# A mixture-of-experts pipeline on one core: halves joined plane by plane, swish read from PSUM, hid turned one step behind its product, and a counter for each product

## The reference

```python
    x = x + 0.5 * _L0_ffn_ref(_layernorm(x), ...)
    x = x + _L0_attn_ref(_layernorm(x), ...)
    x = x + 0.5 * _L0_ffn_ref(_layernorm(x), ...)

def _swiglu(h):
    glu = jnp.minimum(h[..., ::2], LIMIT)          # LIMIT = 7.0
    lin = jnp.clip(h[..., 1::2], -LIMIT, LIMIT)
    return glu * jax.nn.sigmoid(ALPHA * glu) * (lin + 1.0)

# expert block: 32 experts, 4 chosen for each token
        t = _rmsnorm(x, norm_scale)
        g = t @ gate_w.T + gate_b
        vals, idx = jax.lax.top_k(gf, K)
        w = jax.nn.softmax(vals, axis=-1)
        combine = jnp.zeros((T, E)).at[jnp.arange(T)[:, None], idx].add(w)
        h1 = jnp.einsum('th,efh->tef', tf, w1) + b1
        h = _swiglu(h1)
        hw = h * combine[:, :, None]
        out = jnp.einsum('tef,ehf->th', hw, w2) + combine @ b2
        return x + out
```

## Time and profile before

| | us |
|---|---|
| median of 3 runs | 711.7 (710.67 to 713.89) |
| time of the profiled execution | 712.26 |
| its span, first to last instruction | 710.5 |
| POOL busy | 507.7 (71%) |
| PE busy | 504.9 (71%) |
| ACT busy | 455.6 (64%) |
| DVE busy | 436.0 (61%) |

### The profile page before, as it was taken

The page is one execution under the profiler, slowest core; times in us unless marked ns, Lnnn a source line. Parts: engine busy times, 40 slices in busy tenths (PEclk is TensorE's granted clock), DMA queues, the critical chain, the costliest instruction groups (busy, mean ns, idle before and its releaser), DMA issues. The chain is left out here.

```text
span 710.5 us, 11944 instructions
## 1 busy us (share of the span) xinstructions
PE 504.9 (71%) x2868; PEld 408.8 (58%) x2869; DVE 436.0 (61%) x1243; ACT 455.6 (64%) x784; POOL 507.7 (71%) x551
## 2 busy tenths in 40 slices
PE   6258977999979997595507864699997999935000
PEld 3144364889868886264404552388896988834000
DVE  6889232665548778388983877155663787845122
ACT  4848425999879897595807747399986999711000
POOL 3677777777557776777677777777763777777765
PEclk9556999999999999697558955899999999957555
DMA  7998115787569995122121111578766999624222
GB/s 268 394 368 319 52 53 126 194 218 212 183 160 192 223 220 177 45 54 56 45 55 52 53 53 52 112 172 220 206 197 158 206 211 221 178 75 126 66 63 59
DMA packets 144043, 108.25 MB, mean 152 GB/s; under 512 B 112416, under 2 KB 119808, under 8 KB 143872
## 3 DMA queue, kind: packets, MB, share of 16 engines
q1 hardware_dynamic: 127616, 74.14, 39.2%
q0 software_dynamic: 16384, 33.59, 16.4%
HBM read 25.84 MB, written 56.62 MB: 116 GB/s over the span
## 5 line engine op out<-in xcount | busy, mean ns | idle before, releaser
L570 POOL DMA_INDIRECT YG<-ys,row x256 | 247.3, 966 | 104.1 <-issue 98.0
L545 POOL DMA_INDIRECT xs<-planes,row x256 | 249.9, 976 | 81.4 <-issue 71.3
L1321 PE MATMUL PS<-W,xT 128*128 x768 | 192.2, 395 | 17.8 <-ACT xT L659 16.4
L1321 PEld LDWEIGHTS PS<-W,xT 128*128 128x128 f32 x768 | 141.8, 194 | 46.5 <-issue 28.5
L659 ACT ACTIVATE xT<-xP 128x1024 uint16<-128x1024 uint16 x96 | 144.8, 1512 | 36.3 <-DMA xP<-xs 36.2
L1019 DVE TENSOR_SCALAR glulin<-PS 128x512 f32<-128x512 f32 x96 | 66.3, 691 | 124.2 <-PE PS L1330 70.6
L1330 PEld LDWEIGHTS PS<-W,hidT 128*128 128x128 f32 x768 | 99.9, 191 | 6.1 <-issue 1.6
L1330 PE MATMUL PS<-W,hidT 128*128 x768 | 101.7, 276 | 0.5 <-issue 0.5
L650 ACT ACTIVATE swish<-glulin 128x512 f32<-128x512 f32 x96 | 60.4, 629 | 23.1 <-DVE glulin L1019 17.9
L1032 DVE SCALAR_TENSOR_TENSOR hid<-glulin,swish 128x512 f32<-128x512 f32 x96 | 66.4, 692 | 11.9 <-ACT swish L650 5.6
L1024 DVE TENSOR_SCALAR glulin<-PS 128x512 f32<-128x512 f32 x96 | 65.3, 681 | 0.0
(11 more groups left out here) (178 smaller groups left out, 690.1 us busy)
## 6 DMA issues: line engine op xcount, KB each, us to landing
ys<-yrow SPq DMA_DIRECT2D x96, 256.0 KB
xs<-YG SPq DMA_DIRECT2D x6, 2048.0 KB, 14.0
W<-in_w12T SPq DMA_DIRECT2D x1, 6144.0 KB, 34.4
xs<-planes,row POOLq DMA_INDIRECT x256
YG<-ys,row POOLq DMA_INDIRECT x256, 2.5
out<-X SPq DMA_DIRECT2D x7, 256.0 KB, 2.5
xP<-xs SPq DMA_TRANSPOSE x96
X<-in_x SPq DMA_DIRECT2D x4, 256.0 KB, 3.3
```

The source lines that it names most:

```text
L545: pool.indirect_dma_start(out=xs[c].bitcast(U16), out_offset=bass.IndirectOffsetOnAxis(ap=row[:, i:i + 1], axis=0), in_=planes[:, (c * CT ...
L570: pool.indirect_dma_start(out=YG[:, t * TOPK + k, :], out_offset=None, in_=ys[c], in_offset=bass.IndirectOffsetOnAxis(ap=row[:, i:i + 1], ...
L1321: last = te.matmul(h1, xT[:, r, q * P:(q + 1) * P], W[:, bass.ds(es[q], 2 * H)], start=True, stop=True)
```

## The change

- **Join.** The copy that puts the halves together walks through all low halves of the 512 numbers and then through all high halves. Before, it took the low and the high half of each number in turn.
- **Swish.** ACT reads the first product in PSUM itself and computes the swish of the unbounded number. The bound is put on the result: DVE takes the smaller of swish and `cap`, which holds the swish of 7, in the instruction that makes `hid`. So `glu` is gone, DVE does two instructions for a group in place of three. `lin` waits until the swish has read, and `hid` waits for `lin`. The 1 that is added to `lin` is folded into the bias b1 once at the start, and the bounds are -6 and 8.
- **Order.** PE does in step k: first product of k-1, turn of k-2, second product of k-3. ACT does: y copy of k-4, join of k, swish of k-1, copy to `hidT` of k-2. SP's order, `STORE_LAG` and the waits of its loads and stores stay as they are.
- **Counts.** `h1_ready` counts first products and `y_ready` second products, in place of `multiplied` and `seam_multiplied`. ACT and DVE can read the first product before the second product of the same step is done.
- At the start of the first block ACT computes `cap`, and the load of its table goes with it. The loops of DVE are cut in another way, with the same work in each step.

The core of the diff:

```diff
@@ scalar, experts @@
                 def copy_y(n, r, m):
+                    act.wait_ge(y_ready, n + (g0 + 1))
                     wait_count(act, yrow_stored[r], (m + (g0 // 2)) * 16)
                     a.activation(yrow[:, r, :], YP[r], ACT.Copy).then_inc(yrow_ready, 1)
 
                 def swish_of(n, r):
-                    act.wait_ge(glu_ready, n + (g0 + 1))
+                    act.wait_ge(h1_ready, n + (g0 + 1))
                     wait_count(act, hid_ready, n + (g0 - 1))
-                    a.activation(swish[:, r, :], glu[:, r, :], ACT.Gelu_apprx_sigmoid).then_inc(swish_ready, 1)
+                    a.activation(swish[:, r, :].rearrange("p (q f) -> p q f", q=GT),
+                                 H1[r].rearrange("p (q g f) -> p g q f", q=GT, g=2)[:, 0],
+                                 ACT.Gelu_apprx_sigmoid).then_inc(swish_ready, 1)
 
                 def copy_hid(n, r):
                     act.wait_ge(turned, n + (g0 + 1))
+                    wait_count(act, y_ready, n + (g0 - 1))
                     a.activation(hidT[:, r, :], HT[r], ACT.Copy).then_inc(hidT_ready, 1)
...
-                    wait_count(act, multiplied, n + (m0 - 1))
-                    a.activation(xT[:, r, :].bitcast(U16).rearrange("p (q n w) -> p q n w", q=GT, w=2),
-                                 xP[:, r, :].rearrange("p (w n q) -> p q n w", q=GT, w=2), ACT.Copy).then_inc(xT_ready, 1)
+                    wait_count(act, h1_ready, n + (g0 - 1))
+                    a.activation(xT[:, r, :].bitcast(U16).rearrange("p (q n w) -> p w q n", q=GT, w=2),
+                                 xP[:, r, :].rearrange("p (w n q) -> p w q n", q=GT, w=2), ACT.Copy).then_inc(xT_ready, 1)
...
-                    if live(k, 5, NGF) and not (isinstance(k, int) and NG + 3 <= k <= NG + 4):
-                        act.wait_ge(multiplied, k + (m0 - 1))
-                        copy_y(k - 5, s, m - (3 if r == 0 else 2))
-                    if live(k, 2, NGF):
-                        swish_of(k - 2, r)
-                    if live(k, 3, NGF):
-                        wait_count(act, multiplied, k + (m0 - 1))
-                        copy_hid(k - 3, s)
-                    join_rows(k, r, m)
+                    behind_seam = isinstance(k, int) and k > NG
+                    if live(k, 4, NGF) and not (behind_seam and k - 4 < NG):
+                        copy_y(k - 4, r, m - 2)
+                    if live(k, 0, NGF) and not (isinstance(k, int) and k == NG + 1):
+                        join(k, r, m)
+                    if live(k, 1, NGF):
+                        swish_of(k - 1, s)
+                    if live(k, 2, NGF) and not (behind_seam and k - 2 < NG):
+                        copy_hid(k - 2, r)
@@ vector, experts @@
-                        dve.wait_ge(multiplied, k + m0)
-                        wait_count(dve, swish_ready, k + (g0 - 2))
-                        v.tensor_scalar(glu[:, s, :].rearrange("p (q f) -> p q f", q=GT), h1[:, 0],
-                                        LIMIT, None, ALU.min).then_inc(glu_ready, 1)
+                        dve.wait_ge(swish_ready, k + g0)
+                        wait_count(dve, hid_ready, k + (g0 - 2))
+                        v.tensor_scalar(lin[:, s, :].rearrange("p (q f) -> p q f", q=GT), h1[:, 1],
+                                        1 - LIMIT, 1 + LIMIT, ALU.max, ALU.min).then_inc(lin_ready, 1)
                     add(1)
                     if live(k, 1, NGF):
-                        wait_count(dve, hid_ready, k + (g0 - 2))
-                        v.tensor_scalar(lin[:, s, :].rearrange("p (q f) -> p q f", q=GT), h1[:, 1],
-                                        -LIMIT, LIMIT, ALU.max, ALU.min).then_inc(lin_ready, 1)
+                        dve.wait_ge(lin_ready, k + g0)
+                        wait_count(dve, turned, k + (g0 - 2))
+                        v.scalar_tensor_tensor(hid[:, s, :], swish[:, s, :], cap[:, 0:1], lin[:, s, :], ALU.min, ALU.mult)\
+                            .then_inc(hid_ready, 1)
@@ tensor, experts @@
                 def step(k, r):
-                    if live(k, 3, NGF):
-                        turn_hid(k - 3, 1 - r)
+                    s = 1 - r
+                    behind_seam = isinstance(k, int) and k > NG
                     if live(k, 1, NGF):
-                        last = first_product(k - 1, 1 - r)
-                        if live(k, 4, NGF) and not (isinstance(k, int) and k == NG + 3):
-                            last = second_product(k - 4, r)
-                        last.then_inc(multiplied, 1)
+                        first_product(k - 1, s)
+                    if live(k, 2, NGF) and not (behind_seam and k - 2 < NG):
+                        turn_hid(k - 2, r)
+                    if live(k, 3, NGF) and not (behind_seam and k - 3 < NG):
+                        second_product(k - 3, s)
```

More of the change, by code:

```diff
@@ L719, in experts @@
                         step(i * 4 + (8 + j), j % 2, i * 2 + (8 + j) // 2)
[L720 to L721 removed]
+                drain(NG)
+                join(NG, 0, NG // 2)
+                join(NG + 1, 1, NG // 2)
+                for k in range(NG + 1, NG + 8):
                     step(k, k % 2, k // 2)
```

114 lines of the change are left out of this document (35 added, 79 removed).

## The result

The changed kernel takes 718.07 us (median of 6 runs, 717.61 to 721.3), the kernel before 711.85 (710.53 to 713.89). The ratio is 1.0086, with a 95% interval of 1.0068 to 1.0104: slower by 6.2 us. The prediction was 712.0 with a range from 707.4 to 717.0; the measured time lies above it. What happened is in the main what its second rival described, the store as the new wait, with a part of the third, a join that gets less short than taken. The profiled execution took 717.92 us, with a span of 716.2.

A forecast was written before the change was run, and what follows sets the result against it. POOL's indirect DMAs were taken as the bound, so only its waits, 4.1 us, could be had. Block 1 0.1 us earlier and block 2 0.2 later made +0.1: 711.8, given as 712.0 us, range 707.4 to 717.0.

The forecast's parts named there:

- second rival: Y copy's store becomes the new wait: at 3.4 us a step, 5.1 us more, 716.8 us; chance 0.21.
- third rival: Join on ACT doesn't get shorter, its 16-bit output being stepped: 3.4 to 3.5 us a step, 717 to 720 us; chance 0.07.
- limit of 4.1 us from the four gaps: POOL's waits before gathers 0 to 3: most that faster experts can bring, 2.66 + 0.86 + 0.59 = 4.1 us.
- an earlier end of the experts changes nothing there: First block's seam, before gather 0: stores land behind loads that wait for scatter 1, so no gain there.
- limit of 0.86 us: Second block's seam, before gather 2: a wait of 10.33 us against 9.47, so at most 0.86 us can be had.
- gap before gather 0: POOL's wait at the first seam: unchanged at 9.5 us; a move of over 1 us would make the whole reading wrong.
- the sum: Second half-stages: 1.5 us gained minus 21 times the step's growth; with the second seam's 0.86, +0.1 us together.
- first rival: Stores land in time, steps of 3.15 us or less, gathers 1 and 3 without a gap: 4.1 us less, 707.6; chance 0.22.
- `yrow` ring: Two-step loop of join, load, store issue, landing and y copy: 6.6 us, 3.28 a step in the second half-stages.
- In the first half-stages 3.1 to 3.2: Pace of the experts' steps in each block's first half-stage, claimed at 3.1 to 3.2 us a step.
- fill and drain: Start and end of a half-stage: 0.5 us less at the start and 1.0 us less at the end.
- The path from a first product to `hid` stays as long: Swish part: swish, lin, hid in place of glu, swish, hid, claimed equally long, and begun earlier by the second product.

The follow-up runs named there:

- a_lag5: The changed kernel with STORE_LAG 5 in place of 6, each store issued one group earlier: 710.81 us, ratio 0.9948 to the kernel before.
- a_storefirst_4: The changed kernel with SP issuing the store of k-6 ahead of the load of k, fourth try: 710.36 us, ratio 0.9966 to the kernel before.
- a_best_3: The changed kernel with four yrow buffers, STORE_LAG 5 and POOL's wait for xT_ready one group back, third try: 709.99 us, ratio 0.9966 to the kernel before.
- j_steps: The changed kernel with 21 more copies on ACT before its first step, in seven access patterns: plain 1.051 us, the new join's 1.343, the old join's 1.504.
- a_y4: The changed kernel with four yrow buffers in place of two, order and STORE_LAG 6 kept: 711.25 us, ratio 0.9952 to the kernel before.

## Why the prediction was wrong

**What bounds the kernel.** Right in the main thing: no version gained more than 4.3 us by its ratio (3.4 by its median), near the limit of 4.1 us from the four gaps, and a_lag5 closed the gaps before gathers 1 and 3 to 0.30. One-sided at the seams: "an earlier end of the experts changes nothing there" holds, but a later one costs its whole length beyond the 0.6 us that the experts had to spare. For the second seam the limit of 0.86 us was too tight: the gap before gather 2 fell from 10.33 to 8.8 in a_storefirst_4 and to 8.4 in a_best_3. The prediction named a change of over 1 us in the gap before gather 0 as a sign that the reading is wrong as a whole. The gap grew by 1.94. What was wrong is this one half of it: the sum has no term for late experts in the first half-stages. It also has small slips that don't change the outcome: a landing of 3.3 us makes a step of 3.32 and not 3.29, the first rival is 707.6 in one place and 707.4 in another, and 3.5 a step in the third rival makes 721 and not 720.

**The join, the first step that failed.** I took 1.06 us, bounds 1.06 and 1.51, and said that the two-element run is what differs. It took 1.355: the row L624 has a stepped input and a contiguous output, the new join a stepped output, and that costs 0.29 us by j_steps. The two-element run alone, with input steps of 2 bytes, costs only 0.12. So the reason of the third rival ("its 16-bit output is now stepped", 0.07) was right, and its size was not: the join got shorter by 0.16 of the 0.45 us. By the prediction's own sum of the `yrow` ring, 0.29 more over two steps is 0.15 a step; 42 steps of the second half-stages make 6.2 us, and 712.0 would have been 718.2. That this meets the measured total is half chance: the steps in question grew by less, and the rest came from where the sum had nothing, as the next points show. The rule of the Trainium skill (SBUF — State Buffer, Door 1) of two hits in each 16-byte line nearly held for the input: 8-byte steps, two 16-bit numbers in a line, cost 0.06 us. For the output it doesn't give the price: 4-byte steps have four in a line and cost 0.29.

**The ring of `yrow`.** Its mechanism was right: the number of buffers, the lag of the store, SP's order and the join were each changed, and each moved the time in the direction that the ring says. It was the second rival, with 0.21. The second half-stages got 3.34 and 3.35 where I had 3.28, less than the 3.43 that the dearer join would give in that sum. The landing wasn't too long: where the y copy waited for its store, it took 3.4 us in the mean, from the start of the store's issue (2.4 to 5.3). But the y copy waited in only 25 of the 48 steps of these half-stages. The sum took one landing for every step, and the measured pace is a mean of steps with and without the wait. With 3.34 and 3.35 in the rival's formula, 21 x (0.126 + 0.191) - 3.0 - 0.86, the time grows by 2.8 us and no more.

**The first half-stages, the second step that failed.** "In the first half-stages 3.1 to 3.2": they had 3.30 and 3.26. Out of the first of them came the 3.57 us by which gather 0 starts late, the larger part of the whole; I had given this pace no price.

Term by term, from the timelines: in block 1 the loads of the second chunk came 3.38 us late (in the sum: nothing), 21 steps of 0.124 more made 2.6 (1.4), and fill and drain together gave back 1.5 (1.5). Gather 1 should start 4.5 later, and it did. In block 2 the loads came 3.76 late (538.61 against 534.85), nearly all of it carried over from block 1, 21 steps of 0.191 more made 4.0 (2.5), and fill and drain gave back 2.3 (1.5): 5.5, as measured. The sum expected the loads there 0.86 earlier. So fill and drain were no mistake; the late seams and the step of the second half-stages were.

**Swish from PSUM.** "The path from a first product to `hid` stays as long" was true only of the new order: there the median from the end of a first product to that of `hid` is 2.28 us, against 2.21 from the last product that `multiplied` stood behind. In the old one the swish part costs 0.67%. As a part of the change as a whole it seems to have done no harm (a_y4), but I had counted the instructions in the path and not what they had run beside.

**ACT no longer the bound, DVE's time worth nothing.** ACT had 49 to 51 of 60 us, DVE two instructions for a group in place of three, and the time didn't fall for it; right. POOL's early gains could be kept, as its timeline in a_lag5 shows.

## What to carry to other kernels

When a step of a software pipeline is moved one stage nearer, look at who frees its buffer and behind what that release is queued: here the y copy lost a step of distance to its store, while the DMA queue kept issuing the store behind a load that waits for the instruction behind the y copy. A line or two of the queue's lag or one more pair of buffers was worth more than the whole rewrite, and the new join alone in the old order gave as much as any of them. Where one wait ends only 0.6 us ahead of another that hides it, price its getting later as well as its getting earlier. And price a strided copy by a row with the same step on the same side, input or output.

## What the runs showed of the hardware that I had not expected

A copy of 1024 16-bit numbers for each partition on ACT takes 1.05 us with an output written in order, whether the input steps by 2 or 4 bytes, 1.11 with input steps of 8, but 1.34 with output steps of 4 bytes (j_steps). Taking two planes in turn costs 0.12 us more than plain with input steps of 2 bytes and 0.45 with 8. DVE's multiplication with a bound from a one-column operand takes 0.752 us for 512 columns, against 0.692 for the one with an immediate number (L1005, and L1032 in the earlier trace rows; the two differ in their first operation too). And the same kernel can take 712 us at one time and 875 at another, with the versions of the two orders that were run there ranked the other way; the cause is open.
